# Overflow rows of a mixture-of-experts stage: from blocks of 128 rows to parts of 32, four parts to a group

## The reference

```
x = h.reshape(-1, 256)                      # 1600 rows
assignments = argmax(x @ router_w, axis=-1) # one expert of 14 for each row
weights = softmax(x @ router_w)[assignments]
hid = gelu(x @ w1[e] + b1[e])               # w1[e]: 256 x 512, e = the row's expert
sel = hid @ w2[e] + b2[e]                   # w2[e]: 512 x 256
x = layernorm(x + sel * weights)
```

## Time and profile before

| | |
|---|---|
| median of 3 runs | 512.77 us (511.94 to 515.41) |
| the profiled execution | 515.03 us |
| its span | 513.3 us |
| PE busy | 466.4 us, 91% |
| DVE busy | 345.9 us, 67% |
| ACT busy | 308.9 us, 60% |
| POOL busy | 217.1 us, 42% |
| mean granted TensorE clock | 0.966 |

### The profile page before, as it was taken

How to read it: one execution, slowest core, us unless ns; L and a number is a source line. 1 busy time by engine, 2 the same in 40 slices (tenths; PEclk the granted TensorE clock), 3 DMA queues, 4 the chain that set the end, 5 groups by cost and what they waited for, 6 DMA issues and landing times.

```text
span 513.3 us, 12715 instructions
## 1 busy us (share of the span) xinstructions
PE 466.4 (91%) x4461; PEld 400.7 (78%) x4461; DVE 345.9 (67%) x967; ACT 308.9 (60%) x1404; POOL 217.1 (42%) x299
## 2 busy tenths in 40 slices
PE   3687799998999999999999999989999998899991
PEld 2375587886877988878878978878889887899981
DVE  2779648856769767897578597685366636665653
ACT  2366647776768877877468585776475683333340
POOL 1365424462435544553236246543143432254443
PEclk9879789999999999999999999999999998999997
DMA  5762124435141323543151414060151393699900
GB/s 163 198 156 69 45 93 149 183 115 180 33 170 58 121 85 127 184 128 155 43 178 32 172 33 175 20 216 10 37 169 49 90 349 124 179 378 373 358 31 17
DMA packets 43804, 69.83 MB, mean 136 GB/s; under 512 B 12297, under 2 KB 33914, under 8 KB 43021
## 3 DMA queue, kind: packets, MB, share of 16 engines
q1 hardware_dynamic: 40344, 39.81, 24.8%
q10 hardware_dynamic: 926, 25.83, 13.5%
q0 software_dynamic: 2464, 3.31, 2.1%
HBM read 59.08 MB, written 29.77 MB: 173 GB/s over the span
## 4 chain that ended last, share of the span: by engine, by line
PE 71%; DVE 14%; DMA 6%; issue 3%; ACT 3%; POOL 2%; SPq 1%; DVEq 0%; POOLq 0%; ACTq 0%
PE bank L1418 26%; PE bank L1635 8%; PE bank L1492 7%; PE bank L1830 5%; PE bank L1819 5%; PE bank L1624 5%; PE bank L1664 4%; PE bank L1656 2%; PE bank L1601 2%; DMA vX<-v_tile 2%; DMA out_bias<-in_L_attn_out_b_dram 2%; ACT probs L1094 2%; DVE qk L1200 2%; PE bank L1451 2%; DVE rot L1198 2%
## 5 line engine op out<-in xcount | busy, mean ns | idle before, releaser
L1094 ACT ACTIVATE probs<-bank,neg_max 100x100 f32<-100x100 f32 x512 | 170.1, 369 | 35.6 <-DVE neg_max L1230 27.2
L996 POOL TENSOR_TENSOR probs<-probs,row_inv 100x400 f32<-100x400 f32 x128 | 112.7, 901 | 105.3 <-DVE row_inv L1235 105.1
L1094 ACT ACTIVATION_READ_ACCUMULATOR probs<-bank,neg_max 100x1 f32 x512 | 118.0, 230 | 0.0
L1230 DVE TENSOR_REDUCE neg_max<-bank 100x4 f32<-100x400 f32 x128 | 68.6, 564 | 10.8 <-PE bank L1624 5.4
L1635 PE MATMUL bank<-ident,probs 100*100 100x100 f32 x512 | 68.3, 256 | 6.3 <-POOL probs L996 4.6
L1635 PEld LDWEIGHTS bank<-ident,probs 100*100 100x100 f32 x512 | 51.0, 130 | 18.2 <-POOL probs L996 6.6
L1103 ACT COPY probsT<-bank 100x400 f32<-100x400 f32 x62 | 30.8, 496 | 42.5 <-PE bank L1635 36.5
L1242 DVE COPY probsT<-bank 100x400 f32<-100x400 f32 x66 | 37.6, 570 | 23.0 <-PE bank L1635 17.3
L1418 PE MATMUL bank<-cT_h,W_K 128*128 128x250 f32 (+1 forms) x224 | 46.6, 293 | 4.3 <-DVE kX L1157 1.7
L1492 PE MATMUL bank<-yT,W_Q 128*128 128x250 f32 (+1 forms) x224 | 50.1, 366 | 0.0
L1418 PE MATMUL bank<-W_O,oX_h 128*125 128x256 f32 (+1 forms) x224 | 43.8, 296 | 0.7 <-DVE oX_l L1252 0.7
(11 more groups left out here) (185 smaller groups left out, 964.9 us busy)
## 6 DMA issues: line engine op xcount, KB each, us to landing
expert_rows<-c_empty ACTq DMA_DIRECT2D x13, 1935.0 KB, 8.8
w<-in_L_ffn_w_dram SPq DMA_DIRECT2D x36, 512.0 KB, 7.3
vX<-v_tile SPq DMA_DIRECT2D x14, 200.0 KB
vX<-v_tile SPq DMA_DIRECT2D x12, 150.0 KB
xs<-in_x_dram SPq DMA_DIRECT2D x12, 125.0 KB
vX<-v_tile SPq DMA_DIRECT2D x12, 100.0 KB
kX<-in_L_xattn_WK_dram SPq DMA_DIRECT2D x2, 512.0 KB, 9.8
qX<-in_L_xattn_WV_dram SPq DMA_DIRECT2D x2, 512.0 KB, 6.4
```

Of the source, the lines that this page charges most:

```text
L996: probs_ready.mark(pool.tensor_tensor(v, v, r, ALU.mult), step)
L1094: i = act.activation(probs[:, k % SLOTS, w], sc_bank[p % 2 * 2 + u][0:T, w], ACT.Exp, bias=neg_max[:, k % SLOTS, h:h + 1], accum_out=row_s ...
L1230: max_ready.mark(dve.tensor_reduce(neg_max[:, k % SLOTS, :], src, AX_X, ALU.max, negate=True), step)
```

## The change

Overflow rows are cut into parts of 32 (SUB) instead of blocks of 128. Four parts (LANES), which may belong to four different experts, make a group that takes the place of a block: n = 14 and 15 are groups and always run, later groups run in pairs behind the condition. With the counts above there are 2 + 1 + 3 + 2 = 8 parts, which is two groups, so that no later pair is entered. One row more for the last of them would make nine parts.

- The table has MORE = 48 possible parts in place of 14 blocks, and has more steps: from the expert and number of every part DVE works out, for each of the 128 partitions of a group, the row to fetch (`from_row`) and the expert (`from_expert`).
- POOL fetches the rows, b1 and b2 of a group with three indirect gathers of 128 rows (258, 512 and 256 values each). For group 14 they follow the stores of blocks 4, 5 and 6, for group 15 those of blocks 7, 8 and 9. All three signal one semaphore, `group_in[n % 2]`, and `x_of(n)` asks for all three of them; turn_x(n) waits for that.
- SP loads for each group four w1 and then four w2, by the expert of each part. It waits for fc2(3) before those of group 14 and for fc2(7) before those of group 15, since they go where w1 and w2 of experts 0 to 3 and 4 to 7 were.
- fc1 of a group has the rows as the stationary operand, 32 columns for each part, and the part's w1 as the moving one, 512 columns. The four parts go to four strips of 32 columns. The result has the rows in partitions, so b1 is added by DVE (`add_group_bias`), gelu is one piece (`gelu_group`), and PE turns the result (`turn_h`, four transposes) before ACT copies it (`take_h`) and fc2 follows, again in four strips.
- PE's order at the end is fc1(13), turn_x(15), fc2(12), fc1(14), fc2(13), turn_h(14), fc1(15), fc2(14), turn_h(15), fc2(15).
- DVE adds b1 of group 14 after the statistics of block 12 and before its scaling, and b1 of group 15 likewise in block 13.

The core of the diff:

```
-MORE = (B * T - 1) // P + 2
+SUB = 32
+LANES = P // SUB
+MORE = -(-((B * T - P) // SUB + 2) // LANES) * LANES
...
+        return xg[:, n % 2, :], group_in[n % 2], 3 * 16 * ((n - NE) // 2 + 1)
+    def group_slots(n):
+        return [LANES * (n % 2) + j for j in range(LANES)]
...
+        def load_weights(n):
+            if n < ALWAYS:
+                sp.wait_ge(fc2_ready, group_slots(n)[-1] + 1)
...
+            for e, k in zip(experts, group_slots(n)):
+                sp.dma_start(w1s[k][:, :, :], w1[bass.ds(e, 1)]...).then_inc(group_w1_in[n % 2], 16)
+            for e, k in zip(experts, group_slots(n)):
+                sp.dma_start(w2s[k][:, :, :], w2[bass.ds(e, 1)]...).then_inc(group_w2_in[n % 2], 16)
...
+                pe.wait_ge(group_w1_in[n % 2], LANES * 16 * ((n - NE) // 2 + 1))
+                pe.wait_ge(xT_taken, n + 1 - SEALED)
+                for c in range(KC):
+                    for j, k in enumerate(group_slots(n)):
+                        lane = slice(SUB * j, SUB * (j + 1))
+                        i = pe.matmul(h_bank[n % 2][lane, 0:F], xTs[:, n % SLOTS_X, c, lane], w1s[k][:, c, :],
+                                      start=(c == 0), stop=(c == KC - 1), skip_group_check=True)
...
+        def turn_h(n):
+            pe.wait_ge(group_gelu, n - NE + 1)
+            if n > NE:
+                pe.wait_ge(gelu_ready, n)
             for f in range(FT):
+                i = pe.transpose(turn_bank[:, f * P:(f + 1) * P], hg[:, n % 2, f * P:(f + 1) * P], ident[:, :])
...
+                for f in range(FT):
+                    for j, k in enumerate(group_slots(n)):
+                        lane = slice(SUB * j, SUB * (j + 1))
+                        i = pe.matmul(y_bank[n % 2][lane, 0:D], hT[:, n % SLOTS_X, f, lane], w2s[k][:, f, :],
+                                      start=(f == 0), stop=(f == FT - 1), skip_group_check=True)
...
+        def group_pair(n):
+            turn_h(n)
+            fc1(n + 1)
+            fc2(n)
+            turn_h(n + 1)
+            fc2(n + 1)
...
+        def gelu_group(n):
+            act.wait_ge(group_biased, n - NE + 1)
+            act.activation(hg[:, n % 2, :], hg[:, n % 2, :], ACT.Gelu).then_inc(group_gelu, 1)
+        def take_h(n):
+            act.wait_ge(group_turned, n - NE + 1)
+            act.copy(hT[:, n % SLOTS_X, :, :].rearrange("p f t -> p (f t)"), turn_bank[:, :]).then_inc(gelu_ready, 1)
...
+            pool.indirect_dma_start(out=dst[:, n % 2, :], out_offset=None, in_=table, in_offset=...,
+                                    bounds_check=last, oob_is_err=False).then_inc(group_in[n % 2], 16)
+        first_gather = SEALED + 2
+        wanted = [(n, what) for n in range(NE, ALWAYS) for what in ("x", "b1", "b2")]
+        for n in range(ALWAYS):
+            finish(n)
+            if 0 <= n - first_gather < len(wanted):
+                gather(*wanted[n - first_gather])
...
+        link(dve.tensor_scalar(expert_c[:, :], expert_f[:, :], float(NE - 1), None, ALU.min))
+        link(dve.scalar_tensor_tensor(out=home_f[:, :], in0=expert_f[:, :], scalar=float(CAP // SUB), in1=nth_f[:, :], op0=ALU.mult, op1=ALU.add))
+        link(dve.tensor_tensor(lane_expert[:, :, :], expert_c[:, :].rearrange("p (g j) -> p g j", j=LANES), mine, ALU.mult))
+        link(dve.tensor_tensor(lane_home[:, :, :], home_f[:, :].rearrange("p (g j) -> p g j", j=LANES), mine, ALU.mult))
+        link(dve.tensor_reduce(from_expert_f[:, :], lane_expert[:, :, :], AX_X, ALU.add))
+        link(dve.tensor_reduce(from_part[:, :], lane_home[:, :, :], AX_X, ALU.add))
+        dve.tensor_copy(from_expert[:, :], from_expert_f[:, :]).then_inc(more_ready, 1)
+        dve.scalar_tensor_tensor(out=from_row[:, :], ...).then_inc(more_ready, 1)
...
+        for n in range(ALWAYS):
+            start_norm(n)
+            if NE - 2 <= n < NE:
+                add_group_bias(n + 2)
+            end_norm(n)
```

More of the change, by code:

```diff
@@ L1742, in experts_block @@
     count_bank = bank[6]
+    turn_bank = bank[7]
     def x_of(n):
@@ L1848, in _ @@
                     turn_x(n)
-                run(list(range(first, first + OB)), lambda n: ())
+                fc1(first)
+                group_pair(first)
     @block.scalar
@@ L1912, in _, with finish @@
-        run(list(range(ALWAYS)))
-        pool.wait_ge(more_ready, 3)
+        def finish(n):
+            x, s, count = x_of(n)
+            pool.wait_ge(ve_ready, n + 1)
+            pool.tensor_tensor(rs[:, n % 2, :], ve[:, n % 2, :], half_power[:, :], ALU.pow).then_inc(rs_ready, 1)
+            pool.wait_ge(s, count)
+            pool.wait_ge(res_ready, n + 1)
+            pool.indirect_dma_start(out=flat, out_offset=bass.IndirectOffsetOnAxis(ap=x[:, D + 1:ROW].bitcast(I32), axis=0),
+                                    in_=res[n % SLOTS_R][:, :], in_offset=None, bounds_check=B * T - 1, oob_is_err=False).then_inc(out_stored[n % SLOTS_R], 16)
@@ new lines, in gather @@
+        def gather(n, what):
+            g = n - NE
+            dst, table, index, last = {"x": (xg, rows, from_row, (NE + 1) * CAP - 1), "b1": (b1g, b1, from_expert, NE - 1), "b2": (b2g, b2, from_expert, NE - 1)}[what]
+            pool.wait_ge(more_ready, 4)
+            if n >= ALWAYS:
+                pool.wait_ge(res_ready, n - 1)
+                pool.wait_ge(out_stored[(n - 2) % SLOTS_R], 16 * ((n - 2) // SLOTS_R + 1))
+            pool.indirect_dma_start(out=dst[:, n % 2, :], out_offset=None, in_=table, in_offset=bass.IndirectOffsetOnAxis(ap=index[:, g:g + 1], axis=0),
+                                    bounds_check=last, oob_is_err=False).then_inc(group_in[n % 2], 16)
@@ L1914, in _ @@
+        first_gather = SEALED + 2
[4 more added lines that the diff above has]
+                gather(*wanted[n - first_gather])
+        pool.wait_ge(more_ready, 4)
         for first in LATER:
             with pool.If(in_use(pool, first)):
-                run(list(range(first, first + OB)))
+                for n in range(first, first + OB):
+                    for what in ("x", "b1", "b2"):
+                        gather(n, what)
+                for n in range(first, first + OB):
+                    finish(n)
@@ new lines, in start_norm @@
+        def start_norm(n):
+            s = n % 2
+            x, loaded, count = x_of(n)
+            if n >= SEALED:
+                add_bias(n)
+            dve.wait_ge(loaded, count)
+            dve.wait_ge(y_free, n + 1)
+            dve.scalar_tensor_tensor(out=summed[:, s, :], in0=biased[:, s, :], scalar=x[:, D:D + 1], in1=x[:, 0:D],
+                                     op0=ALU.mult, op1=ALU.add).then_inc(y_summed, 1)
+            dve.wait_ge(y_summed, n + 1)
+            dve.bn_stats(st[:, s, :], summed[:, s, :]).then_inc(st_ready, 1)
+            dve.wait_ge(st_ready, n + 1)
+            dve.tensor_copy(waiter[0:1, 0:1], st[0:1, s, 0:1])
+            dve.bn_aggr(mv[:, s, :], st[:, s, :]).then_inc(mv_ready, 1)
+            dve.wait_ge(mv_ready, n + 1)
+            dve.tensor_scalar(ve[:, s, :], mv[:, s, 1:2], EPS, None, ALU.add).then_inc(ve_ready, 1)
@@ L1990, in _ @@
         for first in LATER:
             with dve.If(in_use(dve, first)):
-                run(list(range(first, first + OB)))
+                for n in range(first, first + OB):
+                    add_group_bias(n)
+                for n in range(first, first + OB):
+                    start_norm(n)
+                    end_norm(n)
 _INS = ["x", "ctx_1024", "_lenS2", "L0_attn_qkv_w", "L0_attn_qkv_b", "L0_attn_out_w", "L0_attn_out_b",
```

198 lines of the change are left out of this document (88 added, 110 removed).

## The result

The changed kernel takes **517.84 us** (median of 6 runs, 516.77 to 518.63) against 512.67 us of the kernel before on the same chip (6 runs, 510.87 to 515.41): ratio **1.0114 [1.0086, 1.0143]**, slower by a little over one per cent. Its profiled execution took 517.57 us, with a span of 515.8 us and a mean granted clock of 0.967.

What follows compares the result with a forecast made beforehand. PE was taken to bound the expert stage, then POOL's gathers and the landing before turn_x(15). Terms ended at 519.4 against the span's 513.3; + 6.1 on the 512.77 median gave 518.9 us, range 511.5 to 526.5.

Steps and rivals of the forecast that it cites:

- The table: DVE's larger table and six more chained steps move its first norm by + 4.2 us (3.5 to 5).
- PE's early wait, fc2(4): fc2(4) on PE, behind DVE's later bias add, starts at about 455.8; PE runs 1.7 us late from there.
- The gathers on POOL: Six gathers behind stores 4 to 9, 1.5 us each (1.0 to 2.4); POOL's period goes from 2.99 to 4.5 us.
- The landing and the wait that decides: Group 15's b2 lands 6.0 us after it starts, at 495.2; PE idles 8 us before turn_x(15).
- Rival 1: Gathers cheap or landing sooner, so turn_x(15) isn't held and weights decide: 515.9, or 514.2 with clock up; chance 0.22.
- The clock: PE's granted clock falls after the 8 us idle, slowing fc2(12) and fc1(14): + 1.75 us (0 to 11.2).
- The strips: A group's fc1 or fc2 in four column strips on PE takes 2.1 us, a gain of a factor of 3.3.
- The tail: Store and what follows behind the last norm unchanged at 5.9 us, less 0.2 for a small copy that falls away.
- The weights: DMA full until about 500.1, when w2 of group 15 lands; all weights in time, the tightest by 6.6 us.
- Rival 3: Strips don't overlap with 512 columns; four products on the chain at 6.92 instead of 2.1 us: 538; chance 0.04.
- Rival 4: Weights come late through a slower stream beside the gathers, deciding from 6.6 us of delay on: 520 to 526; chance 0.04.
- Rival 5: Faster by over 1%, with both bounds, gathers and weights, wrong: 505; chance 0.04.

Runs made afterwards that it cites:

- Experiment 3: Changed kernel with DVE's table worked out for 16 possible parts instead of 48: 515.06 us, ratio 1.0074 to the kernel before.
- experiment 1: Changed kernel with a semaphore of its own for the rows of x, so turn_x no longer waits for b1 and b2: 514.08 us, ratio 1.0055.
- experiment 6: Changed kernel with the later pairs' conditions nested on every engine, so one jump skips all: 516.16 us, ratio 1.0101.
- Experiment 2: Changed kernel with the six gathers behind the stores of blocks 2 to 7 instead of 4 to 9: 513.20 us, ratio 1.0037.
- experiment 4: Changed kernel with 48 unused transposes on PE ahead of turn_x(15), to keep it busy through the wait: 518.64 us, ratio 1.0147.
- experiments 7: Experiment 2's kernel with DVE adding b1 of group 14 one block earlier: 513.49 us, ratio 1.0040.
- experiment 9: Also e9: changed kernel with the edits of experiments 1, 2, 6 and 7 together, all weights loaded: 511.62 us, ratio 0.9991.
- experiment 5: Changed kernel with the group products' inner loops exchanged, all products of a strip in a row: 524.44 us, ratio 1.0257.
- experiments 11: Experiment 9's kernel with b1 and b2 loaded by SP in plain transfers, POOL gathering x only: 515.98 us, ratio 1.0084.
- experiments 12: Experiment 11's kernel with group 15's weights loaded once for each of its two experts: 512.66 us, ratio 1.0006.
- e11: The kernel of experiment 8, with group 15's weights loaded once for each of its two experts: 512.99 us, ratio 1.0044.
- e10: Kernel before with only the conditions of its six later pairs nested: 510.39 us, ratio 0.9981.
- experiment 8: Experiment 7's kernel with group 15's weights loaded once for each of two experts, leaving out that parts 2 and 4 could belong to others: 512.99 us, ratio 1.0044.

## Why the prediction was right, point by point

**The table.** Forecast + 4.2 us, measured + 4.0: 8.29 us from `over` to the first `summed`, where the kernel before took 445.98 - 441.70 = 4.28. Experiment 3 confirms it as a term of the sum: 3.1 us of table were 3.1 us of stage. A 672-element operation takes 0.85 us, 0.49 over the 0.36 of the earlier trace rows, exactly as scaled.

**PE's early wait, fc2(4).** Forecast 1.7 us late, measured a wait of 1.98. In this execution the clock fell behind it, which the working didn't have: 0.75 in 455 to 460, and fc2(4) takes 2.3 us from start to start for 1.73, the fc1 behind it 2.96 for 1.78. So PE is due at turn_x(15) 3.7 us later than in the kernel before, counted from the table's start (45.8 and 42.1 us). The working's terms give 483.79 + 1.7 = 485.5; the "about 487" that it went on with has no row behind it. The fall is no rule: ten other kernels here have a wait of 1.46 to 2.06 us at the same place, and in none of them does the clock leave 1.00. The wait of experiment 1, and the clock around it (it is 1.00 in 455 to 460 too):

```profile
451.91 1.97 PE L1857 MATMUL bank<-w,hT 128*128 128x256 f32 x8 [2.06 <-DVE biased L2006]
```

```profile
450.00:455.00 5.00, 3.09 (x20) 2.91 (x21) 2.93 (x10) 1.07 (x5) 2.57 (x4) 1.00 1.07 372
```

Whether it falls costs nothing in the end, since PE waits again at turn_x(15): 7.50 us in experiment 3, without the short wait, and 8.02 in experiment 6, with it but without the fall.

**The gathers on POOL.** Forecast 1.5 us, measured 0.30 + 1.04 = 1.34, a period of 4.33 instead of 4.47. Power 10 comes 37.9 us after power 0, by forecast 38.7. Experiment 2 shows this as the core: moving them, not removing them, recovers most of the loss (1.0114 to 1.0037).

**The landing and the wait that decides.** Forecast 6.0 us, measured 5.57. PE waits 6.42 us and not 8: from the table's start the landing came at 52.2 us for 53.5, and PE was due at 45.8. By the Trainium skill, DMA: Bandwidth & Descriptors, "Anatomy of one DMA", an estimate of the landing would be 2.3 us; beside a full DMA (share 1.05 in 485 to 490) the trace disagrees, as the earlier trace rows had said. Experiment 1 took this wait away and found the next one some 6 us behind it, so that only a part came back: 2.1 us between the powers and 2.7 in the stage. Rival 1 had about 3.0 for a cheap landing, with the same limit behind it, DVE.

**The clock.** Forecast + 1.75, measured 3.41 - 1.73 = 1.68 in fc2(12), and experiment 4 gives 1.9 for it.

**The strips.** A term that was mis-sized: 2.1 us each, measured 1.73 to 1.98 on the chain, and 1.74 from the start of fc1(15) to the start of fc2(14). The factor of 3.3 of the 100-column row was too low for these products: the 6.92 us in a row over 1.73 give a factor of 4.0. The Trainium skill, TensorEngine Tiling (Array Packing), "Theoretical Speedup" has up to that factor, and this trace agrees. The chain got 8.4 - 7.54 = 0.9 us of it, the rest going into a slow turn_x(15) (0.69 for 0.22) and hand-overs.

**The tail.** Forecast 5.7 us from the end of the last `res`, measured 515.8 - 509.1 = 6.7. I had called it unchanged. In the changed kernel PE finishes its products so near the end that its five jumps outlast ACT's tests by 0.6 us. Experiment 4 shows it most plainly, since ACT's tests are over 4 us before the end there and only PE's jumps are left; experiment 6 fits, but spares ACT's tests too. I had put this term at no change from the rows of a kernel whose span ACT's tests end: no part of my working looked at what PE's sequencer does behind the last product.

**The weights.** Forecast to be in time by 6.6 us. The last w2 landed at 499.9 and was needed at 504.0, a margin of 4.1. Counted from the table's start it came at 61.4 us, where I had 500.1 - 441.7 = 58.4: 3.0 us late. Right for this kernel, and no further: as soon as the gathers were out of the way (experiments 7 and 9) the weights were the bound.

**The sum.** From the table's start to the end I had 519.4 - 441.7 = 77.7 us and the trace has 77.3. The terms are off by - 0.2 (table), - 1.1 (gathers and landing), - 0.2 (PE to fc2(15)) and + 1.0 (tail): the sum was better than its parts, as the tail made up for the gathers, and that is luck. Against the medians the + 6.1 was + 5.2. The ratio's interval reaches from 0.9 to 1.4 per cent, on both sides of the bound I had named, and 517.84 us lies on it (517.9), so on which side of one per cent the kernel falls was luck too. The mechanism, POOL's gathers and the landing behind them that PE waits for, is what the trace and experiments 1 and 2 show.

**The rivals.** Rival 1 was the nearest, and its price for a cheap landing was about right; and its condition, 1 us saved on gathers and landing, was met by a hair (1.1); the tail took the 1.0 back, which left the time at the bound. Rival 3 (no overlap) is refuted by the 1.73, though experiment 5 shows that an order of products exists in which it is half true. Rival 4 (weights late) didn't happen here and did in experiments 7, 9, 11 and 12. Rival 5 needed both bounds off; experiment 9 shows why it stayed out of reach.

**Open.** Why the stage and the medians differ by up to 2 us for some kernels (e11, e9, e10) was not settled; the variable start of the stage is a candidate and was only seen, not tested. Experiments 8 and 6 together (54.2 and 5.4) would give a stage of 9.8 + 54.2 + 5.4 = 69.4, level with e10's 69.5, an estimate from two rows of the table that was not run, and for a kernel that leaves out what experiment 8 leaves out. Open too is why PE's jumps differ so much in length, and why the clock fell behind PE's short wait in the changed kernel alone.

## What to carry to other kernels

When work moves from a full engine to one with 0.74 us of slack a block, price it where it stands in that engine's order: six gathers of 1.34 us placed two blocks earlier cost 4.8 us less than the same six placed late. Before changing a step, list the bounds that come after it (here the wait for the landing, then the bias add behind POOL, then the weights, then PE's jumps at the end): with four mends together the kernel was level with the one before. And look at what the sequencers do behind the last product, because the chain and the busy rows leave branches out.

## What the runs showed of the hardware that was not expected

- A branch of PE over a block that isn't entered, 60 unrolled products long, took 1.9 us at the median and 0.2 to 3.0 us in the changed kernel; over five such blocks at once 3.7 us. A branch of ACT, over its own shorter block, took 45 ns. Five tests of ACT one after another take about 0.46 us each.
- Products in four column strips overlapped by a factor of 4.0 when the strip changes with each product (two records), equally with four records in a row on one strip, and by 1.5 with eight in a row (fc2: 1.73, then 4.5 us). What sets the limit between four and eight was not tried; the two also differ in columns, 512 and 256.
- The same short wait of PE did not always end alike: 1.98 us in the changed kernel was followed by a granted clock of 0.75 in 455 to 460, and ten waits of 1.46 to 2.06 us at the same place in other kernels by 1.00. Waits of 2.44 and 2.83 us (experiments 2 and 4) left it at 1.00; after 4.08 and 6.42 us it was 0.50.
- A gather of 128 rows of 1 or 2 KB occupies POOL for 1.04 us and 0.30 us before it, whatever the rows' size; beside a full DMA it lands in 5.6 to 6.6 us.
- With rows spread over 32 partitions by plain transfers in flight, DMA was at a share of 1.07 to 1.09 and moved 266 to 275 GB/s (experiment 11); without them it moved 386 and 387 (experiment 9).
